# A DLRM tower on one core: one slot ahead of each group of sums is copied out of PSUM by ScalarE and multiplied in place by VectorE; sums one slot later

## What is computed

```python
e = jnp.stack([tbl_0[ids[:, 0]], ..., tbl_39[ids[:, 39]]], axis=1)      # 512 x 40 x 64
viW = jnp.einsum('bpd,pde->bpe', e[:, i_idx, :], W)
z = jnp.einsum('bpe,bpe->bp', viW, e[:, j_idx, :])                      # 512 x 780
h = jnp.concatenate([z, dense_ctx], axis=1)
h = jnp.maximum(h @ W_top1 + b_top1, 0.0)
h = jnp.maximum(h @ W_top2 + b_top2, 0.0)
y = h @ W_top3
```

## Time and profile before

| | |
|---|---|
| median of 3 runs | 352.34 us (351.97 to 353.12) |
| the profiled execution | 352.86 us |
| its span, first to last instruction | 351.0 us |
| TensorE (PE) busy | 340.6 us, 97% |
| VectorE (DVE) busy | 263.7 us, 75% |
| GpSimd (POOL) busy | 226.9 us, 65% |
| ScalarE (ACT) busy | 76.7 us, 22% |
| granted TensorE clock | 1.0 (2.4 GHz) in every slice |

### The profile page before, as it was taken

One profiled execution on the slowest core, in us unless ns is written; L12 is line 12 of the kernel. 1 busy time (PEld: TensorE's weight loads), 2 busy tenths in 40 slices (PEclk: granted clock), 3 DMA queues, 4 the chain that ended last, 5 costly groups with the idle time before them and its releaser, 6 DMA issues.

```text
span 351.0 us, 4414 instructions
## 1 busy us (share of the span) xinstructions
PE 340.6 (97%) x1730; PEld 117.2 (33%) x1730; DVE 263.7 (75%) x252; ACT 76.7 (22%) x118; POOL 226.9 (65%) x176
## 2 busy tenths in 40 slices
PE   7988989999999999999999999999999999999997
PEld 3333343333323233333333333333233333334342
DVE  3887997797867787789889987898998989970010
ACT  1475823223403030303040302103031030000011
POOL 5665466556566566268886879888889999970000
PEclk9999999999999999999999999999999999999999
DMA  7645231221221221822112220222120000000000
GB/s 201 253 138 184 94 112 48 84 75 24 84 74 26 82 78 40 328 82 75 43 41 71 75 77 15 69 68 75 62 67 8 2 0 0 2 0 0 0 2 1
DMA packets 10743, 24.20 MB, mean 69 GB/s; under 512 B 3538, under 2 KB 4306, under 8 KB 10595
## 3 DMA queue, kind: packets, MB, share of 16 engines
q1 hardware_dynamic: 6482, 19.72, 16.3%
q0 software_dynamic: 4096, 4.20, 5.1%
q10 hardware_dynamic: 144, 0.00, 0.0%
HBM read 23.91 MB, written 0.00 MB: 68 GB/s over the span
## 4 chain that ended last, share of the span: by engine, by line
PE 93%; DVE 3%; ACT 3%; issue 1%
PE u L468 52%; PE zp L489 19%; PE u L499 7%; PE xp L443 5%; PE xp L426 3%; PE u L456 2%; PE u L507 2%; PE u L535 2%; ACT xq L397 1%; DVE prod L589 1%; ACT xt L392 0%; DVE xq L567 0%; DVE late L550 0%; DVE prod L554 0%; ACT prod L379 0%
## 5 line engine op out<-in xcount | busy, mean ns | idle before, releaser
L589 DVE TENSOR_TENSOR prod<-u,xq 128x1024 f32<-128x1024 f32 x180 | 206.8, 1216 | 41.3 <-PE u L468 37.1
L468 PE MATMUL u<-xt,w_ring 64*128 64x512 f32 x760 | 190.7, 620 | 2.6 <-ACT xt L392 1.6
L345 POOL DMA_INDIRECT gath<-in_tbl,ids_sb x128 | 123.8, 967 | 76.9 <-DMA gath<-in_tbl,ids_sb 43.4
L353 POOL TENSOR_TENSOR prod<-prod 128x1024 f32<-128x1024 f32 x44 | 102.9, 2365 | 9.3 <-DVE prod L589 9.0
L468 PEld LDWEIGHTS u<-xt,w_ring 64*128 64x128 f32 x760 | 63.8, 185 | 118.5 <-DVE prod L589 64.6
L489 PE MATMUL zp<-prod,sel_sb 128*32 128x512 f32 x604 | 72.5, 597 | 0.0
L397 ACT ACTIVATE xq<-xt 32x512 f32<-32x512 f32 x80 | 50.3, 629 | 2.1
L392 ACT ACTIVATE xt<-xp 128x512 f32<-128x512 f32 x20 | 12.0, 598 | 176.4 <-PE xp L426 150.8
L489 PEld LDWEIGHTS zp<-prod,sel_sb 128*32 128x32 f32 x604 | 17.5, 109 | 51.1 <-issue 46.0
L567 DVE TENSOR_SCALAR xq<-late,row_sb 128x1024 bf16<-128x1024 int32 (+1 forms) x32 | 22.3, 756 | 5.4 <-DMA late<-in_ids_small 4.5
L499 PE MATMUL u<-late 128*128 128x512 f32 x56 | 24.6, 596 | 0.0
(11 more groups left out here) (28 smaller groups left out, 62.1 us busy)
## 6 DMA issues: line engine op xcount, KB each, us to landing
w_ring<-in_w_cell SPq DMA_DIRECT2D x24, 512.0 KB
late<-in_ids_small SPq DMA_DIRECT2D x4, 512.0 KB, 5.1
gath<-in_tbl,ids_sb POOLq DMA_INDIRECT x128
late<-in_w_top SPq DMA_DIRECT2D x1, 1792.0 KB
late<-in_small SPq DMA_DIRECT2D x3, 512.0 KB
late<-in_small SPq DMA_DIRECT2D x2, 256.0 KB
late<-in_w_top SPq DMA_DIRECT2D x1, 512.0 KB
wd_sb<-in_w_diag SPq DMA_DIRECT2D x1, 320.0 KB
```

What stands on the lines that cost most here:

```text
L345: pool.indirect_dma_start(gath[:, g % GR, t, half, :], None, tables[f], bass.IndirectOffsetOnAxis(ap=ids_sb[:, t, f:f + 1], axis=0),).then ...
L353: pool.tensor_tensor(prod[:, lo % PR, :, :], prod[:, lo % PR, :, :], prod[:, hi % PR, :, :], ALU.add).then_inc(folded, 1)
L468: mm = pe.matmul(u[:, n % UR, a, :], w_ring[rows, q % RW, at * P:(at + 1) * P], xt[rows, moving % XR, :], start=True, stop=True)
L589: dve.tensor_tensor(prod[:, n % PR, :, :], u[:, n % UR, :, :], x, ALU.mult).then_inc(prod_ready, 1)
```

## The change

Three things change.

**The sum slot.** `LAG` goes from 3 to 4. The 11 groups without a folded batch that were summed directly after slots 8, 14, 20, 28, 34, 42, 50, 56, 64, 72 and 78 are now summed after 9, 15, 21, 29, 35, 43, 51, 57, 65, 73 and 79. The other groups keep their slot (89, 97, 105, 115, 123, 131, 135, 145, 153, 161, 169, 175, 183, 191, 199, and the end), since there a folded batch decides.

**The staged slot.** For each sum slot s from 30 on, slot s-3 is "staged" if it is a unit. That holds for 20 slots: 32, 40, 54, 62, 76, 86, 94, 102, 112, 120, 128, 132, 142, 150, 158, 166, 172, 180, 188 and 196. ScalarE copies a staged slot's 128x1024 numbers from PSUM to its `prod` buffer. This copy, not a product, frees the PSUM buffer for the fill of slot s. VectorE passes over the staged slot and goes on with s-2, s-1 and s. Then it multiplies the staged slot in place, in SBUF.

**ScalarE's order.** It is now written out slot by slot. The four quarter copies of an item come one per slot, from the slot after `item_slot` on, and the staged copy stands behind those of its own slot.

```diff
-LAG = 3
+LAG = 4
+STAGED_FROM = 30
...
+STAGED_BACK = (3,)
+STAGED = sorted({s - back for s in SUM_SLOT if STAGED_FROM <= s < NS for back in STAGED_BACK if SLOTS[s - back][0] == "unit"})
+
+def dve_order():
+    order = []
+    for n in range(NS):
+        if n not in STAGED:
+            order.append(n)
+        if n in SUM_SLOT:
+            order += [a for a in STAGED if a not in order and a < n]
+    return order
...
             def fold(k, q):
-                pool.wait_ge(prod_ready, PRODS[hi + 1])
+                pool.wait_ge(prod_ready, max(DONE[lo], DONE[hi]))
...
+            def stage(n):
+                act.wait_ge(u_filled, n + 1)
+                act.wait_ge(summed, SLOT_BATCH[n - PR] + 1)
+                act.activation(prod[:, n % PR, :, :], u[:, n % UR, :, :], ACT.Copy).then_inc(staged, 1)
...
+            def wait_free(n):
+                if n in STAGED:
+                    pe.wait_ge(staged, STAGED.index(n) + 1)
+                else:
+                    pe.wait_ge(prod_ready, DONE[n])
...
             def fill(n):
                 if n >= UR:
-                    pe.wait_ge(prod_ready, PRODS[n - UR + 1])
+                    wait_free(n - UR)
...
             def multiply(n):
-                dve.wait_ge(u_filled, n + 1)
-                if n >= PR:
-                    dve.wait_ge(summed, SLOT_BATCH[n - PR] + 1)
+                if n in STAGED:
+                    dve.wait_ge(staged, STAGED.index(n) + 1)
+                else:
+                    dve.wait_ge(u_filled, n + 1)
+                    if n >= PR:
+                        dve.wait_ge(summed, SLOT_BATCH[n - PR] + 1)
...
-                dve.tensor_tensor(prod[:, n % PR, :, :], u[:, n % UR, :, :], x, ALU.mult).then_inc(prod_ready, 1)
+                of = prod[:, n % PR, :, :] if n in STAGED else u[:, n % UR, :, :]
+                dve.tensor_tensor(prod[:, n % PR, :, :], of, x, ALU.mult).then_inc(prod_ready, 1)
```

More of the change, by code:

```diff
@@ L172, with batch_done @@
 DENSE_ROW = (NZ - 1) * P + P - DENSE
-PRODS = [0]
-for _s in SLOTS:
-    PRODS.append(PRODS[-1] + (2 if _s[0] == "diag" else 1))
+STAGED_BACK = (3,)
[8 more added lines that the diff above has]
+    return order
+DVE_ORDER = dve_order()
+DONE, _done = {}, 0
+for _n in DVE_ORDER:
+    _done += 2 if SLOTS[_n][0] == "diag" else 1
+    DONE[_n] = _done
+def batch_done(b):
+    return max(DONE[n] for n, batch in SLOT_BATCH.items() if batch == b)
 def item_slot(k):
@@ L188, in look_up_slot, with xq_slot @@
     return 0 if k < 4 else item_slot(k) - 2
+def xq_slot(k, c):
+    return item_slot(k) + (1 + c if k >= 6 else 0)
 W1_AT = 12
@@ L269, in program @@
         u_filled = sem("u_filled")
+        staged = sem("staged")
         prod_ready = sem("prod_ready")
@@ L381, in cut, with take_rows @@
                 act.activation(parts[s][:, 1, :, :, :], of, ACT.Copy).then_inc(mid_ready, 1)
[L383 to L388, removed]
+            def take_rows(k):
                 act.wait_ge(item_done, k + 1)
                 if k >= XR:
-                    act.wait_ge(prod_ready, PRODS[QUAD_END[(k - XR) // 2] + 1])
+                    end = QUAD_END[(k - XR) // 2]
+                    act.wait_ge(prod_ready, max(DONE[end - 1], DONE[end]))
@@ L392, in _, with take_quarter @@
                 act.activation(xt[:, k % XR, :], xp[:, :], ACT.Copy).then_inc(x_ready, 1)
+            def take_quarter(k, c):
+                h, half = divmod(c, 2)
+                to, of = 64 * (k % 2) + 32 * half, 64 * half + 32 * h
                 act.wait_ge(x_ready, k + 1)
[L394 to L398, removed]
+                act.activation(xq[to:to + 32, k // 2, h, :], xt[of:of + 32, k % XR, :],
+                               ACT.Copy).then_inc(xq_ready, 1)
@@ new lines, in stage @@
+            def stage(n):
+                act.wait_ge(u_filled, n + 1)
+                act.wait_ge(summed, SLOT_BATCH[n - PR] + 1)
+                act.activation(prod[:, n % PR, :, :], u[:, n % UR, :, :], ACT.Copy).then_inc(staged, 1)
+            for n in range(NS):
+                for k in range(NB):
+                    if item_slot(k) == n:
+                        if k in CUT_AT:
+                            cut(CUT_AT[k])
+                        take_rows(k)
+                    for c in range(4):
+                        if xq_slot(k, c) == n:
+                            take_quarter(k, c)
+                if n in STAGED:
+                    stage(n)
+                for t in range(NZ - 1):
+                    if BANK_END_SLOT[t] == n:
+                        take_sums(t)
@@ L399, in _ @@
             for t in range(NZ - 1):
-                if BANK_END_SLOT[t] >= item_slot(NB - 1):
+                if BANK_END_SLOT[t] >= NS:
                     take_sums(t)
@@ L478, in sum_batch @@
                     pe.wait_ge(sel_in, 32)
-                pe.wait_ge(prod_ready, PRODS[batch_last(b) + 1])
+                pe.wait_ge(prod_ready, batch_done(b))
                 if is_folded:
@@ L497, in top_tile @@
                     if t == 0:
-                        pe.wait_ge(prod_ready, PRODS[NS - 2 + m // 2])
+                        wait_free(NS - 3 + m // 2)
                     mm = pe.matmul(h1_ps[m], w1_sb[:, t, m * P:(m + 1) * P], z_sb[:, t, :],
@@ L588, in multiply @@
                 x = x.unsqueeze(1).broadcast_to([P, 2, B])
-                dve.tensor_tensor(prod[:, n % PR, :, :], u[:, n % UR, :, :], x, ALU.mult).then_inc(prod_ready, 1)
+                of = prod[:, n % PR, :, :] if n in STAGED else u[:, n % UR, :, :]
+                dve.tensor_tensor(prod[:, n % PR, :, :], of, x, ALU.mult).then_inc(prod_ready, 1)
             dve.memset(zeros, 0.0).then_inc(warm_ready, 1)
             dve.wait_ge(row_in, 16)
-            for n in range(NS):
+            for n in DVE_ORDER:
                 for s, k in enumerate(SMALL_BLOCKS):
```

## The result

The changed kernel took 358.94 us as the median of 6 runs (355.23 to 360.25), the kernel before 352.15 on the same chip (351.37 to 353.70). The ratio is 1.0168, 95% interval 1.0135 to 1.0201: slower by about 6 us (6.8 by the two medians), where the forecast was 348.4 and its range ended at 355.6. The profiled execution took 360.25 with a span of 358.4, 7.4 more than the span before.

The account below looks back on a forecast made before the run. It took TensorE and VectorE to bound the kernel in turns, through VectorE's products plus its pauses at sums. 352.86 minus 4.6 plus 0.7 is 348.96; the median, 0.52 lower, was forecast at 348.4, range 346.5 to 355.6.

Parts of the forecast that it names:

- The gain at the fill: TensorE's last fill ahead of sums starts after 0.86 us, not 1.13: 0.27 a group, 17 groups, 4.6 us gained.
- the shift: Sums one slot later: four groups get an item directly behind them, costing 0.7 us, bounds 0 and 2.4.
- The pauses: VectorE's waits for a fill at the sums: 1.16 us (24 rows) and 0.30 (16) left behind the staged product.
- cover: VectorE's remaining pause that hides a staged product's delay: 1.16, 0.5 or 0.30 us by group, none at slot 135.
- ScalarE's copy at 1.06: Staged copy from PSUM to SBUF: taken as 1.06 us, bounds 0.60 and 1.20, hidden within 1.94 us available.
- I take no difference: VectorE's staged product with two SBUF inputs: 1.226 us by L550 against 1.216 from PSUM, so no cost.
- the rival: Staged products beside folds wait for the running fold, at most 2.36 us each: 6.5 us lost, 354.9, chance 0.32.
- the port: What VectorE's two-SBUF-input products and GpSimd's folds compete for; 15 of 20 staged products at risk, 6.5 us.
- The folds, which I costed at nothing: GpSimd folds started up to four products later by staging: no cost, being summed ten slots behind their last slot.

Follow-up runs that it names:

- e4: The changed kernel, but each late product reads another slot's PSUM buffer, so it has one SBUF input: 350.39 us, ratio 0.9933 to the kernel before.
- e1: The changed kernel with no staged slot, only sums one slot later and ScalarE's new order: 354.47 us, ratio 1.0073 to the kernel before.
- e11: The changed kernel with late products reading one SBUF input and the first folded group summed two slots later: 347.38 us, ratio 0.9864 to the kernel before.
- e12: The changed kernel with no staged slot and the first folded group summed two slots later: 351.71 us, ratio 0.9996 to the kernel before.
- e10: The changed kernel, but the fold directly ahead of a staged slot also waits for that slot's product: 352.26 us, ratio 1.0007 to the kernel before.
- e13: The changed kernel with the fold ahead of a staged slot waiting for its product, first folded group summed three slots later: 355.37 us, ratio 1.0080 to before.
- e16: The changed kernel with the first folded group summed three slots later and nothing else: 358.97 us, ratio 1.0196 to the kernel before.
- e14: As e13, but two folds ahead of a staged slot wait for its product: 359.81 us, ratio 1.0165 to the kernel before.
- e7: The changed kernel with every GpSimd fold cut into two instructions of 128x512: 361.46 us, ratio 1.0256 to the kernel before.

## Why the prediction was wrong

**The gain at the fill was right.** The step "0.27 us a group, 17 x 0.27 = 4.6" holds: e4 against e1 is 1.40%, 4.9 us, e11 against e12 1.32%, 4.6 us, and the change without folds against before without folds 4.6 (there with 16 gaining groups, and with the shift still in it). The profiles of e11 and e12 show it group by group: e11's lead over e12, taken at the first fill behind each group of sums, grows by 0.27 or 0.28 us at every group with a staged slot, except at 97, 135 and 161, where it does not grow, as forecast. The pauses are nearly as worked out: in e11 1.14 behind slots 88, 112 and 120 (24 rows) and 0.28 behind 102, 150 and 166 (14 or 16), where I had 1.16 and 0.30. Others differ: 0.98 behind 94 and 158, which I gave a cover of 0.5, and 1.84 and 0.90 behind 128 and 142, which I gave 1.16. ScalarE's copy at 1.06 measured 1.023.

**The shift was about right.** "0.7 us" is 0.57 in e1's profiled run (its last group of sums issues at 311.26 instead of 310.69), and e12 shows no difference. That e1's ratio puts it 2.6 above is beyond the term. The move of one sum slot that separates it from e12 points to the first folded group, but no profiled run of e1 shows it late.

**The failing step is the product in place: "I take no difference".** The sum put it at nothing, on the price of L550 (1.226), which had never met a fold, and left the meeting to a rival with a chance of 0.32. The fifteen late products measured 2.05 in the mean instead, up to 4.62, and the 20 cost 12.4 us more than 1.22 each. No row of the kernel before had such a product beside a fold. But the trace did show that 15 of 20 would fall where GpSimd folds 67% of the time. And it had one place where GpSimd issued a gather while L550 ran: the gather took 1.93 us instead of 0.95 and ended 0.82 behind the product:

```profile
21.52 1.23 DVE L550 TENSOR_TENSOR late<-late,prod 128x1024 f32<-128x1024 f32 x1 [1.00 <-ACT prod L379]
21.64 1.93 POOL L345 DMA_INDIRECT gath<-in_tbl,ids_sb  x1 [1.63 <-DMA gath<-in_tbl,ids_sb]
```

The Trainium skill's "SBUF — State Buffer", section "Who interferes with whom", says that such an instruction contends with GpSimd's reads. Every run here agrees with that: 1.214 without folds, up to 5.50 with them, 1.217 with one input from PSUM. What the prediction took from it on top, that the second to issue waits until the first is through, is too little by these runs: slot 166's product, issued at 277.46, also waited for a fold that started at 278.65.

**Inside the rival, the size was too small.** I let a meeting cost what is left of one running fold, 2.36 at most, and had 6.5 us for the port and 354.9. The waits went up to 4.62 - 1.22 = 3.4 us, and the port costs 8.3 to 11.7 us. Three things are missing from that sum. A product can wait for more than one fold, mostly until GpSimd's next fold can't start. That alone adds little: with e11's pauses as cover the eight long products of the change cost about 7.6 us, an estimate, since seven of the fifteen met no fold at all. The folds, which I costed at nothing for their ten slots of margin, come late in their turn and stop the sums, 3.1 us in the change. And behind two stops the clock of the profiled run was at half, 1.7 us each time. So that the rival's mean was only 4 us short is in part luck: some waits were longer than its 2.36, but 8 of the 15 products met a fold, where its sum had 10.

## What to carry to other kernels

Before an operand moves from PSUM to SBUF to free a buffer, count the SBUF inputs of the instruction that then reads it, and what GpSimd does at that time: two inputs beside a stream of ready GpSimd instructions can wait for several of them, not for one. Where the placement must stay, a wait on the GpSimd side, so that it lets go in front of that product, helped here (1.6% in e10 beside the change, 1.2% in e13 beside e16), while shorter GpSimd instructions did not; but each such wait is taken from GpSimd's own margin, and a second one lost it all again (e14). And an engine that is made earlier meets the next chain that does not move with it; ask which one before the gain is booked.

## What was not expected of the hardware

- GpSimd passed the port from instruction to instruction while a VectorE product waited: three more halves of 1.25 us in e7, one more whole fold in the change, mostly up to a fold that had to wait for a semaphore, or up to a gather. Twice in e7 the product got in between.
- The contention also works the other way on gathers. While a product of two SBUF inputs ran (226.18 to 227.40 in the change), an indirect DMA that takes 0.94 took 1.79 on GpSimd's queue; the product itself took its 1.22:

```profile
226.18 1.22 DVE L645 TENSOR_TENSOR prod<-prod,xq 128x1024 f32<-128x1024 f32 x1
...
226.42 1.79 POOL L373 DMA_INDIRECT gath<-in_tbl,ids_sb  x1 [0.30 <-issue]
```

- The length of a stop of TensorE did not tell whether the granted clock falls to its lower level behind it. It did behind stops of 2.37 and 2.64 us in the change and 2.01 in e10. It stayed at 1.0 behind the same 2.64 in e16, behind 2.07 in e13, and behind 0.68 inside the sums of slot 153 in e10 (250 to 262 of that run).
